# A Mamba-2 layer on one Trainium2 chip: in the scan over chunks, PSUM is read two and four banks at a time and five kinds of copies move from VectorE to ScalarE

## What is computed

```python
z, xBC, dt = split(xn @ in_proj_w.T)
x, B, C = split(silu(conv(xBC)))            # x: 64 heads of 64, B and C: 128 wide
dt = clip(softplus(dt + dt_bias), 0, 100)
X = x * dt;  Adt = dt * -exp(A_log)
A_cum = cumsum(Adt)                          # within a chunk
Y_diag = einsum(C, B, exp(segsum(Adt)), X)   # inside a chunk, lower triangle
states = einsum(B, exp(A_cum[-1] - A_cum), X)
Y_off = einsum(C, prev_states, exp(A_cum))
y = Y_diag + Y_off + x * D
y = norm_w * (y * rsqrt(mean(y*y) + eps)) * silu(z)
out = y @ out_proj_w.T
```

## Time and profile before

| | us |
|---|---|
| median of 2 runs | 7035.14 |
| the two runs | 6971.07 and 7099.22 |
| profiled execution, its own time | 6878.64 |
| its span, slowest core (core 3) | 6876.8 |
| spans of the eight cores | 6794.2 to 6876.8 |
| TensorE matmul busy | 4526.2 (66%) |
| VectorE busy | 2156.8 (31%) |
| ScalarE busy | 619.7 (9%) |
| GpSimd busy | 330.0 (5%) |

### The profile page before, as it was taken

One profiled execution on the slowest core, in us unless ns is written; L12 is line 12 of the kernel. 1 busy time (PEld: TensorE's weight loads), 2 busy tenths in 40 slices (PEclk: granted clock), 3 DMA queues, 4 the chain that ended last, 5 costly groups with the idle time before them and its releaser, 6 DMA issues.

```text
span 6876.8 us, 53541 instructions; the slowest of 8 cores (6794.2 to 6876.8 us)
## 1 busy us (share of the span) xinstructions
PE 4526.2 (66%) x19944; PEld 1982.3 (29%) x19944; DVE 2156.8 (31%) x2933; ACT 619.7 (9%) x744; POOL 330.0 (5%) x229
## 2 busy tenths in 40 slices
PE   3437777777767777789988885445445445452699
PEld 3312333333223333334433332112112112111244
DVE  4521111111111111110045554444444444452211
ACT  2200000000000000001101001001000100100000
POOL 0000000000000000000000000000000000000000
PEclk6568898889888988899988885555555555555899
DMA  1134444444455544433333331010010010014443
GB/s 57 43 46 52 54 52 51 51 51 76 53 68 61 59 56 56 51 80 75 69 49 51 52 51 27 23 34 20 22 36 20 21 37 20 21 31 95 104 129 120
DMA packets 586240, 365.14 MB, mean 53 GB/s; under 512 B 484881, under 2 KB 550802, under 8 KB 577634
## 3 DMA queue, kind: packets, MB, share of 16 engines
q0 software_dynamic: 374096, 187.25, 22.7%
q1 hardware_dynamic: 211890, 174.47, 9.0%
HBM read 472.59 MB, written 76.32 MB: 80 GB/s over the span
## 4 chain that ended last, share of the span: by engine, by line
PE 54%; DMA 22%; DVE 12%; issue 6%; ACT 2%; another core or an unknown queue 2%; SPq 1%; POOL 1%; DVEq 0%; ACTq 0%; POOLq 0%
DMA wupb<-wupT 14%; PE pb L1121 13%; PE pb L1081 9%; PE pb L365 6%; PE pb L1000 6%; PE pb L398 5%; PE pb L757 5%; PE pb L764 5%; DMA ygt<-ygs 3%; DVE cacc L418 2%; DMA gscr<-stk 2%; DMA arow<-acr 2%; DVE y L806 1%; DVE P L876 1%
## 5 line engine op out<-in xcount | busy, mean ns | idle before, releaser
L1081 PE MATMUL pb<-xnTb,wupb 128*128 128x512 bf16 x4096 | 952.3, 394 | 665.4 <-DMA wupb<-wupT 665.0
L1121 PE MATMUL pb<-wd,h 128*128 128x512 bf16 x4096 | 898.8, 380 | 25.0 <-DVE h L1101 25.0
L1081 PEld LDWEIGHTS pb<-xnTb,wupb 128*128 128x128 bf16 x4096 | 406.3, 101 | 1211.2 <-issue 780.6
L398 PE MATMUL pb<-xnTb,wx 128*128 128x512 bf16 x2176 | 568.1, 430 | 117.2 <-DVE xbcin L407 117.2
L757 PE MATMUL pb<-arow,ones 1*128 1x512 bf16 x768 | 466.9, 608 | 175.8 <-DMA arow<-acr 166.4
L1101 DVE TENSOR_TENSOR h<-h,srow 128x1024 bf16<-128x1024 bf16 x128 | 88.7, 693 | 1541.5 <-ACT h L1094 1541.5
L1121 PEld LDWEIGHTS pb<-wd,h 128*128 128x128 bf16 x4096 | 394.8, 98 | 511.8 <-issue 47.4
L1000 PE MATMUL pb<-wo,ygc 128*128 128x512 bf16 x2048 | 444.3, 380 | 146.5 <-DVE wo L960 146.5
L365 PE MATMUL pb<-wz,xnTb 128*128 128x512 bf16 x2048 | 444.4, 380 | 25.3 <-DMA wz<-winT 25.3
L1142 DVE SCALAR_TENSOR_TENSOR acc<-pb,acc 128x512 bf16<-128x512 f32 x448 | 310.0, 692 | 480.4 <-PE pb L1121 480.4
L1094 ACT ACTIVATE h<-pb,bupc_s 128x512 bf16<-128x512 f32 x256 | 176.5, 689 | 2278.1 <-PE pb L1081 2278.1
(11 more groups left out here) (145 smaller groups left out, 3102.1 us busy)
## 6 DMA issues: line engine op xcount, KB each, us to landing
wd<-wdT POOLq DMA_DIRECT2D x16, 4096.0 KB, 30.0
wupb<-wupT POOLq DMA_DIRECT2D x128, 512.0 KB, 8.3
wx<-winT POOLq DMA_DIRECT2D x34, 512.0 KB, 6.3
xt<-x SPq DMA_DIRECT2D x16, 1024.0 KB
wz<-winT POOLq DMA_DIRECT2D x8, 2048.0 KB, 16.9
zs<-z SPq DMA_DIRECT2D x128, 128.0 KB
xts<-xt SPq DMA_DIRECT2D x32, 512.0 KB
zc<-zs SPq DMA_DIRECT2D x16, 1024.0 KB
```

What stands on the lines that cost most here:

```text
L398: last = e.matmul(pb[bi][:, :], wb[:, :].rearrange("p (k c) -> p k c", k=KT)[:, k], self.xnTb[:, :].rearrange("p (k t) -> p k t", k=KT)[:, ...
L1081: last = e.matmul(pb[bi][:, :], wb[:, :].rearrange("p (k c) -> p k c", k=KT)[:, k], self.xnTb[:, :].rearrange("p (k t) -> p k t", k=KT)[:, ...
L1121: last = e.matmul(pb[bi][:, :], h16[:, j * HT + lt * 128: j * HT + (lt + 1) * 128], wd16[:, :].rearrange("p (j d) -> p j d", j=8)[:, j, ds ...
```

## The change

All of it is in the allocation of PSUM and in phaseB.

- The eight banks become slices of one tensor `psumAll`, so that one instruction can read across banks (`self.pview`).
- The X loop has four groups of 1024 columns in banks 0 and 1. The VectorE instructions are twice as wide, and Xd is read from PSUM with a new factor `dtds` = dt·dstok (one small VectorE instruction for each chunk) in place of Xc.
- `atok`, `btok`, the `Dq` slices, P16 and the `ygs` stages are made by ScalarE, not VectorE. `Dq` becomes Relu(−x) over banks 2 and 3 in one instruction of 1024 columns, and the exponential takes scale −1.
- The four VectorE instructions at L806, L842 and L876 become one of 2048 columns each.
- `ygs` stages hold 1024 columns; four stores of 256 KB replace eight of 128 KB.

```diff
-        self.pbank = [self.ps(f"pb{i}", [128, 512], F32) for i in range(8)]
+        self.psumAll = self.ps("psumAll", [128, 4096], F32)
+        self.pbank = [self.psumAll[:, i * 512:(i + 1) * 512] for i in range(8)]
+        self.pview = self.psumAll
...
-            em.op("dve", lambda e, atok=atok: e.tensor_copy(
-                atok[:, :], pb[0][:, 0:NH]),
+            em.op("act", lambda e, atok=atok: e.activation(
+                atok[:, :], pb[0][:, 0:NH], AF.Copy),
...
+            em.op("dve", lambda e, c=c, dstok=dstok: e.tensor_tensor(
+                self.dtds[:, :], self.dt_tok[:, c * NH:(c + 1) * NH],
+                dstok[:, :], ALU.mult),
...
-            em.op("dve", lambda e: e.tensor_copy(
-                btok[:, :], pb[0][:, 0:128].bitcast(BF16)[:, 0:128]),
+            em.op("act", lambda e: e.activation(
+                btok[:, :], pb[0][:, 0:128].bitcast(BF16)[:, 0:128], AF.Copy),
...
-            for g in range(8):
-                bi2 = g % 2
...
+            for gg in range(4):
+                for sub in range(2):
+                    g = gg * 2 + sub
...
+                      Xc[:, sl].rearrange("p (b h q) -> p b h q", b=2, h=8),
+                      wide4,
...
-                      Xc[:, sl].rearrange("p (h q) -> p h q", h=8),
-                      dstok[:, g * 8:(g + 1) * 8].unsqueeze(2)
-                      .broadcast_to([128, 8, PP]),
+                      wide4,
+                      self.dtds[:, gg * 16:(gg + 1) * 16]
...
-                        em.op("dve", lambda e, cs=cs, bk=bk, db_=db_:
-                              e.tensor_scalar(
-                              db_[:, cs], pb[bk][:, :], 0.0, None, ALU.min),
-                              reads=[r_pb[bk]], writes=[r_db],
+                        em.op("act", lambda e, dd=dd, db_=db_: e.activation(
+                            db_[:, dd * 1024:(dd + 1) * 1024],
+                            self.pview[:, 1024:2048], AF.Relu, scale=-1.0),
+                            reads=[r_pb[2], r_pb[3]], writes=[r_db],
...
-                        mb[:, :], db_[:, :], AF.Exp),
+                        mb[:, :], db_[:, :], AF.Exp, scale=-1.0),
...
-                for n in range(4):
-                    em.op("dve", lambda e, n=n, sl2=sl2, pbank_h=pbank_h:
-                          e.tensor_tensor(
-                          P32[:, sl2], P32[:, sl2], pbank_h[n][:, :], ALU.add),
-                em.op("dve", lambda e, half=half: e.tensor_copy(
+                em.op("dve", lambda e, half=half: e.tensor_tensor(
+                    P32[:, half * 2048:(half + 1) * 2048],
+                    P32[:, half * 2048:(half + 1) * 2048],
+                    self.pview[:, 2048:4096], ALU.add),
+                em.op("act", lambda e, half=half: e.activation(
                     P16[:, half * 2048:(half + 1) * 2048],
-                    P32[:, half * 2048:(half + 1) * 2048]),
+                    P32[:, half * 2048:(half + 1) * 2048], AF.Copy),
...
-                em.op("dve", lambda e, pv=pv, sb_=sb_: e.tensor_copy(
-                    sb_[:, :], pv[:, 0:512]),
-                    reads=[r_pb[bi2]], writes=[r_sb], dbg=f"evyg{c}_{g}")
+                em.op("act", lambda e, pvb=pvb, sb_=sb_: e.activation(
+                    sb_[:, :].rearrange("p (b x) -> p b x", b=2), pvb,
+                    AF.Copy),
+                    reads=[r_pb[0], r_pb[1]], writes=[r_sb],
```

More of the change, by code:

```diff
@@ L582, in phaseB @@
         r_dfull = em.res("dfull")
-        ygstage = [self.sb(f"ygs{b}", [128, 512], BF16, pbs) for b in range(2)]
+        ygstage = [self.sb(f"ygs{b}", [128, 1024], BF16, pbs) for b in range(2)]
         r_ygst = [em.res(f"ygs{b}") for b in range(2)]
@@ L586, in phaseB @@
         r_btok = em.res()
+        self.dtds = self.sb("dtds", [128, NH], BF16, pbs)
+        self.r_dtds = em.res("dtds")
         self.gscr_h = self.dint("gscr", [NCH, NH], F32)
@@ L672, in phaseB @@
                 reads=[r_atok], writes=[r_eatok], dbg="eatok")
+            em.op("dve", lambda e, c=c, dstok=dstok: e.tensor_tensor(
+                self.dtds[:, :], self.dt_tok[:, c * NH:(c + 1) * NH],
+                dstok[:, :], ALU.mult),
+                reads=[self.r_dtok, r_dstok], writes=[self.r_dtds],
+                dbg=f"dtds{c}")
             em.op("sp", lambda e, c=c, stk=stk: e.dma_start(
@@ L735, in phaseB @@
                       ALU.mult),
-                      reads=[r_Xc, r_dstok], writes=[r_Xd], dbg=f"xd{c}_{g}")
+                      reads=[r_pb[0], r_pb[1], self.r_dtds], writes=[r_Xd],
+                      dbg=f"xd{c}_{gg}")
             for half in range(2):
@@ L837, in phaseB @@
                       writes=r_pbh, dbg=f"yd{c}_{half}")
-                for n in range(4):
-                    sl2 = slice(half * 2048 + n * 512,
-                                half * 2048 + (n + 1) * 512)
-                    em.op("dve", lambda e, n=n, sl2=sl2, pbank_h=pbank_h:
-                          e.scalar_tensor_tensor(
-                          y32[:, sl2], pbank_h[n][:, :], 1.0, y32[:, sl2],
-                          ALU.mult, ALU.add),
-                          reads=[r_pbh[n], r_y32], writes=[r_y32],
-                          dbg=f"ev2_{c}_{half}_{n}")
+                em.op("dve", lambda e, half=half: e.scalar_tensor_tensor(
+                    y32[:, half * 2048:(half + 1) * 2048],
+                    self.pview[:, 2048:4096], 1.0,
+                    y32[:, half * 2048:(half + 1) * 2048],
+                    ALU.mult, ALU.add),
+                    reads=r_pbh + [r_y32], writes=[r_y32],
+                    dbg=f"ev2_{c}_{half}")
             for half in range(2):
@@ L925, in phaseB @@
                     reads=[r_sb], writes=[self.r_ygt[c]], dma=True,
-                    dbg=f"styg{c}_{g}")
+                    dbg=f"styg{c}_{gg}")
         if "yg" in self.dbg:
```

174 lines of the change are left out of this document (91 added, 83 removed).

## The result

| | before | changed |
|---|---|---|
| median, us | 6970.09 (10 runs) | 7119.39 (11 runs) |
| lowest and highest, us | 6874.42, 7239.95 | 7097.72, 7241.11 |
| ratio to before, 95% interval | | 1.0331 [1.0293, 1.0369] |
| profiled execution: its time, span | 6878.64, 6876.8 | 7097.72, 7096.1 |

The changed kernel is slower by 3.3%. In some executions the cores of a die run at a lower mean clock; the ratios leave those out, and the profiles of experiments 3, 6 and 10 are of such executions, but in their scan the granted clock is 0.51 to 0.52 on every core, as it is before the change.

A forecast was written before the change was run, and what follows sets the result against it. No engine is full; a chain of hand-overs bounds the kernel, at a chunk's head the DMA chain. Terms (a) to (h) sum to +15.7 us a chunk, +252 over 16 chunks, giving 7255 us, range 7125 to 7420.

The forecast's parts named there:

- (a): Head of a chunk: ScalarE's `btok` queues behind the `gbc` exponential, so the X loop follows the DMA chain; +14.2 us a chunk.
- (b): Output stores of a chunk: four serial stores in place of eight, twice the bytes each; −6.7 us a chunk.
- (c): Before the first output store: eight transposes for four and a longer ScalarE copy start it later; +1.05 us a chunk.
- (d): Decay matrices: TensorE's third `Dq` slice in a quarter waits until ScalarE has read both banks; +4.9 us a chunk.
- (e): Tail of each half, last decay matmul to output matmul: 7.97 us in place of 8.40; −0.86 us a chunk.
- (f): L842 of the second half and both L876: one VectorE instruction for four, 2.29 against 3.07 us; −2.25 a chunk.
- (g): State update, first half: P16 takes 1.91 us on ScalarE against 1.23, with GpSimd waiting; +0.7 us a chunk.
- (h): End of a chunk: the square queues behind both P16 copies on ScalarE, 5.87 us against 1.15; +4.7 us a chunk.
- Over 4 us: Output stores: a store step above 4 us would show the prediction wrong; 2.7 us a step was forecast.
- `btok` in time: Rival, head of a chunk: the X loop stays hidden, +1.5 us a chunk, 7059 us; chance 0.06.
- The clock: Rival, decay stage: the clock rises, 96 matmuls take 20 us less, −4.7 us a chunk, 6960 us; chance 0.04.
- Table loads: Rival, ScalarE in the scan: function switches each need a table load, +190 us more, 7450 us; chance 0.06.

The follow-up runs named there:

- experiment 3: The changed kernel with the square of y emitted ahead of the loop over the state halves; ratio to before 1.0188, a chunk of 141.6 us.
- experiment 6: The changed kernel with `btok` ahead of the `gbc` exponential, square first, second P16 late, `Dq` one bank at a time; ratio to before 0.9726.
- experiment 10: Next chunk's scan and `gscr` store ahead of `ygs` stores, on the changed kernel repaired, with late loads, alternating X-loop banks, split state; median 6756 us.
- Experiment 5: The changed kernel with the `Dq` slices read one bank at a time, still on ScalarE; ratio to before 1.020, a chunk of 139.0 us.
- experiment 1: The changed kernel with `btok` emitted ahead of the `gbc` exponential; ratio to before 0.9999, a chunk of 131.5 us.
- experiment 2: The kernel before with one edit, `btok` copied by ScalarE instead of VectorE; ratio to before 1.0258, a chunk of 143.2 us.

## Why the prediction was right

The forecast was slower, 7255 us within 7125 to 7420, by +15.7 us a chunk and a ratio of 1.037. Measured were 7119.39 us, +15.2 us and 1.033. Direction, chunk and ratio came out as forecast. The absolute number did not: it lies 136 us below the forecast and 5.6 us below the low end of the range. The step that failed there is the base to which the sum was added. I put the forecast midway between what the lower of the two runs shown and their median would give, a base of 7003 us; over ten runs the kernel before has a median of 6970, and the ten spread from 6874 to 7240, so two of them said little. On the profiled execution the same +252 us gave 7131, where 7097.72 were measured.

Term by term. The measured numbers are means of 16 chunks on 8 cores, 128 in all, from the timelines of the two profiles; "quarter" is one of the four of the decay matrices:

| term | predicted | measured | before, after (us) |
|---|---|---|---|
| (a) `btok` behind `gbc` | +14.2 | +14.2 | `gbc` exponential to first decay matmul: 0.14, 14.35 |
| (b) four stores | −6.7 | −6.5 | first store's issue to the x load's: 15.70, 9.22 |
| (c) later first store | +1.05 | +1.0 | first stage transpose to first store: 1.33, 2.33 |
| (d) stop inside a quarter | +4.9 | +4.4 | first quarter to the next 13.04, 14.37; third to the next 12.44, 12.67; second and fourth, first matmul to last, 9.77, 11.18 each |
| (e) tails of the halves | −0.86 | −1.0 | last decay matmul's start to output matmuls: 9.04, 8.55, twice |
| (f) one instruction for four | −2.25 | −2.4 | −0.8 at L842 of the second half, −1.6 at the two L876 |
| (g) first P16 | +0.7 | +0.7 | end of the add to GpSimd: 1.48, 2.15 |
| (h) second P16 and the square | +4.7 | +4.5 | end of the add to the mean: 1.25, 5.76 |

The measured column adds up to +14.9 of the 15.2 us. In (h) the forecast took the start of the P16 copy for the end of the add, 1.15 us in place of 1.25. Experiment 5 took off 6.3 us, more than (d), because it does more than undo it: it also shortens both tails by 0.4 us each, and its third quarter takes 11.3 us where the kernel before took 12.4, since ScalarE is free there and VectorE was not.

(a) is the term on which the sign rested, and experiments 1 and 2 show it from both sides: taken out of the changed kernel it leaves 1.4 of the 15.2 us, put alone into the kernel before it makes 2.6 of the 3.3%. The durations of the wide instructions were right within 0.03 us; the rows of the groups by line and shape in the changed kernel (busy us, mean ns, idle before):

```profile
L793 ACT ACTIVATE Dq<-psumAll 128x1024 f32<-128x1024 f32 x128 | 131.0, 1023 | 1010.8 <-PE psumAll L784 1010.8
L936 ACT ACTIVATE ygs<-psumAll 128x1024 bf16<-128x1024 bf16 x64 | 65.5, 1023 | 174.5 <-PE psumAll L926 158.9 <-DMA ygt<-ygs 15.5
L730 DVE TENSOR_TENSOR Xc<-psumAll,dt_tok 128x1024 bf16<-128x1024 bf16 x64 | 78.4, 1225 | 381.2 <-PE psumAll L718 381.2
L746 DVE TENSOR_TENSOR Xd<-psumAll,dtds 128x1024 bf16<-128x1024 bf16 x64 | 77.8, 1215 | 0.0
L739 DVE TENSOR_TENSOR XD<-psumAll,dfull 128x1024 bf16<-128x1024 bf16 x64 | 43.6, 681 | 0.0
L889 DVE TENSOR_TENSOR P<-P,psumAll 128x2048 f32<-128x2048 f32 x32 | 73.2, 2287 | 127.4 <-POOL P L880 93.9 <-PE psumAll L872 33.5
```

1.02 us for ScalarE's 1024 columns (1.05 forecast), 1.22 for VectorE's Xc and Xd, 0.68 for XD, which keeps its speed over two banks, and 2.29 for 2048 columns. The two unknowns, whether reads across banks run at the old rate and what twice the bytes cost in a store, came out near the values taken: a store step is 2.9 us on the mean (2.65 in the median), 2.7 forecast. Over 4 us, which the prediction names as a sign of being wrong, it is in 19 of 384 steps.

One number in (d) came out by luck. To the third quarter I gave +0.2, saying that TensorE had to wait there anyway, and the mean is +0.23. But it is the mean of two kinds of chunk. TensorE's timeline at the start of the third quarter, in one chunk before and in one after:

```profile
5048.65 0.38 PE L757 MATMUL pb<-arow,ones 1*128 1x512 bf16 x1
5048.87 0.38 PE L764 MATMUL pb<-negHE_s,aB 32*128 32x512 bf16 x1
...
5129.80 0.63 PE L784 MATMUL psumAll<-negHE_s,aB 32*128 32x512 bf16 x1
5130.23 0.63 PE L777 MATMUL psumAll<-arow,ones 1*128 1x512 bf16 x1
```

In the first the matmuls follow each other every 0.22 us, the pace of the 2.4 GHz level, in the second every 0.43, that of the 1.2 GHz level, and either holds for all or nearly all of the first twelve of the quarter; the twelve after the stop run at 0.43. Both levels occur in both kernels. With the fast first half the quarter takes 11.87 us before and 11.97 after, so there the wait was indeed there anyway. With the slow one it takes 12.96 and 14.40: +1.4, the same stop as in the other quarters. The fast kind had 61 of 128 chunks before and 91 of 128 after. With 61 in both the term would have been +0.8. That the change makes the fast kind more frequent is not shown: each count is from one execution, and the profiles of experiments 1 and 5 have 84 and 67.

In (h) a wait was read incompletely. The end of a chunk in the timeline of the changed kernel, against the earlier trace rows:

```profile
5179.82 2.29 DVE L889 TENSOR_TENSOR P<-P,psumAll 128x2048 f32<-128x2048 f32 x1 [5.87 <-POOL P L880]
...
5182.25 1.91 ACT L895 ACTIVATE P<-P 128x2048 bf16<-128x2048 f32 x1 [6.30 <-DVE P L889]
5184.07 3.60 ACT L900 ACTIVATE yg<-y 128x4096 bf16<-128x4096 f32 x1
...
5187.86 0.15 DVE L903 TENSOR_SCALAR stk<-stk 128x1 f32<-128x1 f32 x1 [5.76 <-ACT yg L900]
```

The sum was right: VectorE is idle 5.76 us, 5.87 forecast. But only experiment 3 showed that the second P16 alone, not just the square, stands ahead of the norm's logarithm, so that moving the square does not give the whole term back.

The rivals. *`btok` in time:* the exponential of `gbc` waited 18.66 us, where the earlier trace rows had 17.80, so the X loop was 14 us late and not 0. *The clock:* the granted clock of the decay stage is 0.50 after the change as before, in windows with 8.73 and 9.94 of 10 us busy; the level of 1.2 GHz did not change there. Of the 96 decay matmuls of a chunk only the first twelve of the third quarter ran at the other level, and their larger share after the change is worth 0.6 us a chunk (12.67 for the quarter against 13.24 with the old share), not the rival's 20. The Trainium skill, in "TensorE: Matmul & The Clock Gate" under "What's actually happening", has activity release the throttle; neither trace agrees for these matmuls of 1 and 32 rows in the first quarter. *Table loads:* Copy, Relu, Exp, Ln and Square alternate on ScalarE in the scan, and no load row belongs to it. The nearest row is that of the earlier trace rows, under its new line, in another stage:

```profile
L1355 ACT ACT_TABLE_LOAD x16 | 20.5, 1283 | 228.2 <-PE psumAll L1349 228.2
```

That agrees with the Trainium skill, "ScalarE: Activation LUTs", "Table sets: the hidden batching unit", by which relu and copy are in every set.

## What to carry to other kernels

An instruction moved to an idle engine takes that engine's queue with it: look first at what the instruction ahead of it waits for, and who waits for the moved one. Here 0.26 us behind a DMA wait cost 13 us a chunk. Reading several PSUM banks in one instruction saves the fixed cost (2.29 against 3.07 us for four banks) and is a gain where one operation fills all the banks anyway, and a loss where the producer was filling one bank while the other was read and that place is on the chain (the `Dq` slices, 4.4 us a chunk). A mean over chunks can hide two kinds of chunk, and one chunk can show only one of them: count the kinds before the mean is used.
